# A routed mixture-of-experts stage: x's transposes ahead of the up product, VectorE's order in a step, a smaller block table, and no GpSimd drain at the end

## The reference

```python
x = x + conv_ref(ln_c(x), cfc_w, bn_w, bn_b)       # a gate per image and channel, from mean, max, std and a median
t = to_tokens(x)                                    # 2048 tokens x 512
h = ln_t(t)
logits = h @ router_w.T                             # 8 experts
top_vals, top_idx = top_k(logits, 1)                # one expert for each token
glu = lambda h, wg, wu, wd: silu(h @ wg) * (h @ wu) @ wd
t = t + glu(h, shared_gate.T, shared_up.T, shared_down.T) + sum_e sigmoid(top_vals) * (top_idx == e) * glu(h, w1[e], v1[e], w2[e])
x = from_tokens(t)
```

## Time and profile before

| | us |
|---|---|
| median of three runs | 476.2 |
| span of the profiled execution, first to last instruction | 474.6 |
| TensorE busy | 385.1 |
| VectorE busy | 278.0 |
| ScalarE busy | 160.8 |
| GpSimd busy | 167.9 |

### The profile page before, as it was taken

One profiled execution on the slowest core, in us unless ns is written; L12 is line 12 of the kernel. 1 busy time (PEld: TensorE's weight loads), 2 busy tenths in 40 slices (PEclk: granted clock), 3 DMA queues, 4 the chain that ended last, 5 costly groups with the idle time before them and its releaser, 6 DMA issues.

```text
span 474.6 us, 7391 instructions
## 1 busy us (share of the span) xinstructions
PE 385.1 (81%) x1874; PEld 314.1 (66%) x1875; DVE 278.0 (59%) x499; ACT 160.8 (34%) x262; POOL 167.9 (35%) x203
## 2 busy tenths in 40 slices
PE   2453010389999999999997999999999999999981
PEld 2342010178888888888885778788778788777860
DVE  5985877743645665564679744746447654664330
ACT  4884545221222222232100144515343434343110
POOL 4762911510202022120680658341524152415110
PEclk9655555568999999999999999999999999999997
DMA  8800430110111111111133436974736673633100
GB/s 299 323 1 0 141 124 1 44 46 7 60 44 46 66 44 44 65 46 44 44 113 110 134 120 247 329 247 133 261 107 229 244 265 105 233 151 120 49 24 24
DMA packets 15863, 56.14 MB, mean 118 GB/s; under 512 B 2591, under 2 KB 2591, under 8 KB 12384
## 3 DMA queue, kind: packets, MB, share of 16 engines
q1 hardware_dynamic: 10960, 40.93, 24.0%
q0 software_dynamic: 4880, 14.95, 9.4%
HBM read 43.28 MB, written 13.63 MB: 120 GB/s over the span
## 4 chain that ended last, share of the span: by engine, by line
PE 71%; DVE 13%; issue 5%; ACT 3%; POOL 3%; DVEq 2%; DMA 1%; POOLq 0%
PE GU L1111 41%; PE yb L1111 19%; PE tx L1096 3%; PE th L1103 3%; PE th L1138 3%; DVE tiles L736 2%; DVE search L738 2%; DVEq L247 1%; DVE bn_parts L686 1%; DVE stats L900 1%; DVEq L248 1%; PE yb L1079 1%; PE mb L1089 1%; DVE xT L804 1%; ACT tiles L513 1%
## 5 line engine op out<-in xcount | busy, mean ns | idle before, releaser
L1111 PE MATMUL GU<-w_parts,xT 128*128 (+1 forms) x864 | 220.1, 404 | 4.1 <-issue 2.0
L1111 PEld LDWEIGHTS GU<-w_parts,xT 128*128 128x128 f32 x864 | 160.8, 192 | 41.0 <-issue 9.0
L1111 PE MATMUL yb<-w_parts,hT 128*128 (+1 forms) x432 | 107.3, 397 | 4.9 <-DVE hT L813 4.9
L1111 PEld LDWEIGHTS yb<-w_parts,hT 128*128 128x128 f32 x432 | 79.1, 188 | 22.0 <-issue 6.3
L587 ACT ACTIVATE hT<-th 128x512 fp32r<-128x512 f32 x36 | 21.5, 599 | 171.0 <-PE th L1103 171.0
L448 POOL DMA_INDIRECT out<-x_sb,scatidx x20 | 28.5, 1427 | 104.1 <-DVE x_sb L1010 102.1
L819 DVE TENSOR_TENSOR hidden<-hidden,GU 128x512 f32<-128x512 f32 x36 | 24.8, 688 | 60.5 <-issue 43.6
L577 ACT ACTIVATE xT<-tx 128x512 fp32r<-128x512 f32 x37 | 22.2, 599 | 91.2 <-PE tx L1096 91.2
L501 ACT ACTIVATE w_parts<-w_raw 128x2048 f32 (+1 forms) x27 | 50.7, 1907 | 0.1
L1005 DVE TENSOR_TENSOR w_parts<-w_raw,w_parts 128x2048 f32 x19 | 43.5, 2289 | 6.5 <-ACT w_parts L501 3.0
L404 POOL TENSOR_TENSOR x_rstd<-x_mv,eps 128x1 f32<-128x1 f32 x16 | 3.5, 217 | 117.3 <-DVE x_mv L795 117.3
(11 more groups left out here) (195 smaller groups left out, 386.0 us busy)
## 6 DMA issues: line engine op xcount, KB each, us to landing
w_raw<-weights SPq DMA_DIRECT2D x27, 1024.0 KB, 4.9
x_sb<-x_tok SPq DMA_DIRECT2D x8, 512.0 KB, 7.4
xn_d<-tiles SPq DMA_DIRECT2D x16, 256.0 KB, 2.0
z_d<-x_sb SPq DMA_DIRECT2D x16, 256.0 KB, 2.0
tiles<-xn_d,tokidx POOLq DMA_INDIRECT x21, 4.1
x_sb<-z_d,tokidx POOLq DMA_INDIRECT x20, 5.2
out<-x_sb,scatidx POOLq DMA_INDIRECT x20, 3.8
conv<-conv_par SPq DMA_DIRECT2D x1, 10.0 KB, 9.9
```

What stands on the lines that cost most here:

```text
L1111: last = pe.matmul(dst, left[:, lp, kc, :], wset(q, k, wp, kc), start=(i == 0), stop=(i == 3 * KC - 1))
```

## The change

It does five things.

- `nc.Block(no_gpsimd_drain=True)`.
- TensorE's step: `transpose_x` of block n + 2 moves ahead of the up product of n + 1. The table now gives a set number for this block and the next; slot and counter value are worked out from it in registers (`at % 2`, `at * 3`).
- ScalarE's step: `x_hi` moves ahead of `silu_gate`, and four table entries in place of seven are read behind both. One flag serves GATE and UP.
- VectorE's step: `x_lo` moves ahead of `gated`; three entries in place of seven are read, behind `gated`; the GATE split stands before `add_routed`, the UP split behind it, ahead of DOWN's.
- GpSimd no longer makes the low parts of set 2's gate and up; VectorE makes them between `gated` of block 0 and block 0's step. `block_table` has some instructions fewer.

```diff
-SLOT_COL, READY_COL, SLOT2_COL, READY2_COL = range(4)
-TOTAL_COL = 4
-OTHER_COL, FIRST_COL, LOADED_COL, BEFORE_COL = range(8, 12)
-FLAG_COL, COLS = 12, 16
+SET_COL, SET2_COL, TOTAL_COL = range(3)
+DUE_GU_COL, DUE_DOWN_COL, AT_COL, FIRST_COL, COLS = range(4, 9)
...
-        block = ctx.enter_context(nc.Block())
+        block = ctx.enter_context(nc.Block(no_gpsimd_drain=True))
...
-            return [nc.s_assert_within(v, lowest.get(col, 0), highest.get(col, 1))
-                    for v, col in zip(got, cols)]
+            return [nc.s_assert_within(v, *bounds[col]) if col in bounds else v for v, col in zip(got, cols)]
...
             split_lo(1, DOWN)
-            split_lo(2, GATE)
             pool.wait_ge(z_out, 16 * NT)
             for b in range(RING - 1):
                 gather_z(b)
-            split_lo(2, UP)
             pool.wait_ge(tables, 1)
...
             def step(b, u, j, base):
                 h_hi(b + NT, u % 2)
+                x_hi(b + (NT + 2), u % 2)
                 silu_gate(b + (NT + 1), 1 - u % 2)
-                entries = table_entries(act, b + 1, range(OTHER_COL, FLAG_COL + 3))
-                x_hi(b + (NT + 2), u % 2)
-                next_set(entries)
+                next_set(table_entries(act, b + 1, range(DUE_GU_COL, FIRST_COL + 1)))
...
+            def lo_of(k, at):
+
+                dve.wait_ge(whi, at * 3 + (k + 4))
+                dve.wait_ge(wlo, at * 3 + (k + 3))
+                if isinstance(at, int):
+                    lo, hi = (w_parts[:, (at + 1) % 2, k, part, :, :] for part in (LO, HI))
+                else:
+                    lo, hi = (w_parts[:, ds((at + 1) % 2, 1), k, part, :, :].rearrange("p a k c -> p (a k) c") for part in (LO, HI))
+                dve.tensor_tensor(lo, w_raw[:, k, :, :], hi.bitcast(F32), ALU.subtract).then_inc(wlo, 1)
...
             def step(b, u, j, base):
                 h_lo(b + NT, u % 2)
-                entries = table_entries(dve, b + 1, range(OTHER_COL, FLAG_COL + 3))
+                x_lo(b + (NT + 2), u % 2)
                 gated(b + (NT + 1), 1 - u % 2)
-                x_lo(b + (NT + 2), u % 2)
-                next_set(entries, (GATE, UP))
+                due_gu, due_down, at = table_entries(dve, b + 1, range(DUE_GU_COL, AT_COL + 1))
+                with dve.If(due_gu > 0):
+                    lo_of(GATE, at)
                 add_routed(b + NT, b, u, j * 16 + 16 * (base + 1))
-                next_set(entries, (DOWN,))
+                with dve.If(due_gu > 0):
+                    lo_of(UP, at)
+                with dve.If(due_down > 0):
+                    lo_of(DOWN, at)
...
             dve.wait_ge(tables, 1)
-            next_set(table_entries(dve, 0, range(OTHER_COL, FLAG_COL + 3)), (DOWN,))
+            lo_of(GATE, 1)
+            lo_of(UP, 1)
+            _, due_down, at = table_entries(dve, 0, range(DUE_GU_COL, AT_COL + 1))
+            with dve.If(due_down > 0):
+                lo_of(DOWN, at)
             groups(dve, step, last)
...
-                q, ready, q_after, ready_after = table_entries(pe, b, range(SLOT_COL, READY2_COL + 1))
-                gate_product(n + 1, 1 - u % 2, 1 - u % 2, q_after, ready_after)
+                at, after = table_entries(pe, b, range(SET_COL, SET2_COL + 1))
+                gate_product(n + 1, 1 - u % 2, 1 - u % 2, after % 2, after * 3)
                 transpose_h(n, u % 2)
-                up_product(n + 1, 1 - u % 2, 1 - u % 2, q_after, ready_after)
 
                 pe.wait_ge(xg_in[ahead], j * 16 + 16 * (base + 1 + (u + 2) // RING))
                 transpose_x(n + 2, xg[:, ahead, :])
-                down_product(n, u % 2, q, ready)
+                up_product(n + 1, 1 - u % 2, 1 - u % 2, after % 2, after * 3)
+                down_product(n, u % 2, at % 2, at * 3)
```

More of the change, by code:

```diff
@@ L618, in next_set @@
             def next_set(entries):
[L620 to L626, removed]
+                due_gu, due_down, at, first = entries
+                for ks, due in (((GATE, UP), due_gu), ((DOWN,), due_down)):
+                    with act.If(due > 0):
+                        act.wait_ge(y_done if ks == (DOWN,) else u_done, first + NT)
+                        for k in ks:
+                            act.wait_ge(w_in[k], at * 16 + 32)
+                            split_hi(w_raw[:, k, :, :], w_parts[:, ds((at + 1) % 2, 1), k, HI, :, :].rearrange("p a k c -> p (a k) c"))
             def step(b, u, j, base):
                 h_hi(b + NT, u % 2)
+                x_hi(b + (NT + 2), u % 2)
                 silu_gate(b + (NT + 1), 1 - u % 2)
-                entries = table_entries(act, b + 1, range(OTHER_COL, FLAG_COL + 3))
-                x_hi(b + (NT + 2), u % 2)
-                next_set(entries)
+                next_set(table_entries(act, b + 1, range(DUE_GU_COL, FIRST_COL + 1)))
             def last(b, u, j, base):
@@ L638, in _ @@
             act.wait_ge(tables, 1)
-            next_set(table_entries(act, 0, range(OTHER_COL, FLAG_COL + 3)))
+            next_set(table_entries(act, 0, range(DUE_GU_COL, FIRST_COL + 1)))
             groups(act, step, last)
@@ L977, in block_table @@
                 settle()
-                note(dve.scalar_tensor_tensor(out=ft[:, :, FLAG_COL + GATE], in0=r_b, scalar=0.0, in1=live, op0=ALU.is_equal, op1=ALU.mult))
-                note(dve.scalar_tensor_tensor(out=ft[:, :, FLAG_COL + UP], in0=r_b, scalar=0.0, in1=live, op0=ALU.is_equal, op1=ALU.mult))
+                note(dve.scalar_tensor_tensor(out=ft[:, :, DUE_GU_COL], in0=r_b, scalar=0.0, in1=live, op0=ALU.is_equal, op1=ALU.mult))
                 note(dve.tensor_tensor(fl, fl, r_b, ALU.is_equal))
-                own(dve.tensor_scalar(ei, ei, 1, None, ALU.bitwise_and))
@@ L985, in block_table @@
-                note(dve.memset(ft[:, 0, FLAG_COL:FLAG_COL + 2], 0.0))
-                note(dve.tensor_tensor(ft[:, :, FLAG_COL + DOWN], fl, live, ALU.mult))
-                own(dve.tensor_copy(ft[:, :, OTHER_COL], ei))
-                own(dve.tensor_scalar(ft[:, :, SLOT_COL], ft[:, :, OTHER_COL], -1.0, 1.0, ALU.mult, ALU.add))
-                note(dve.tensor_copy(ft[:, 0:NB - 1, SLOT2_COL:READY2_COL + 1], ft[:, 1:NB, SLOT_COL:READY_COL + 1]))
-                own(dve.tensor_copy(ft[:, NB - 1, SLOT2_COL:READY2_COL + 1], ft[:, NB - 1, SLOT_COL:READY_COL + 1]))
+                note(dve.tensor_copy(ft[:, 0:NB - 1, SET2_COL], ft[:, 1:NB, SET_COL]))
@@ L992, in block_table @@
+                own(dve.tensor_copy(ft[:, NB - 1, SET2_COL:SET2_COL + 1], ft[:, NB - 1, SET_COL:SET_COL + 1]))
+                note(dve.memset(ft[:, 0, DUE_GU_COL:DUE_GU_COL + 1], 0.0))
+                own(dve.tensor_tensor(ft[:, :, DUE_DOWN_COL], fl, live, ALU.mult))
                 note(dve.tensor_copy(tab[0:1, 0:NB, 0:TOTAL_COL + 1], ft[:, :, 0:TOTAL_COL + 1]))
-                own(dve.tensor_copy(tab[0:1, 0:NB, OTHER_COL:FLAG_COL + 3], ft[:, :, OTHER_COL:FLAG_COL + 3]))
+                own(dve.tensor_copy(tab[0:1, 0:NB, DUE_GU_COL:COLS], ft[:, :, DUE_GU_COL:COLS]))
@@ L994, in block_table @@
                 dve.engine_nop().then_inc(tables, 1)
-            def next_set(entries, ks):
-                other, _, _, before, *due = entries
-                for k in ks:
-                    with dve.If(due[k] > 0):
-                        dve.wait_ge(whi, before + (k + 4))
-                        dve.wait_ge(wlo, before + (k + 3))
-                        lo, hi = (w_parts[:, ds(other, 1), k, part, :, :].rearrange("p a k c -> p (a k) c") for part in (LO, HI))
-                        dve.tensor_tensor(lo, w_raw[:, k, :, :], hi.bitcast(F32), ALU.subtract).then_inc(wlo, 1)
+            def lo_of(k, at):
[6 more added lines that the diff above has]
+                dve.tensor_tensor(lo, w_raw[:, k, :, :], hi.bitcast(F32), ALU.subtract).then_inc(wlo, 1)
```

17 lines of the change are left out of this document (6 added, 11 removed).

## The result

The changed kernel takes 463.44 us (median of four runs, 461.75 to 466.02) against 476.04 of the kernel before: ratio 0.9756, interval 0.9721 to 0.9792. The profiled execution has a span of 464.3 us and a time of 466.02, so 1.7 us lie between; the forecast had counted 1.6. The forecast was 466.5 (464.2 to 471.8).

A forecast was written before the change was run, and what follows sets the result against it. TensorE's work was taken as the bound. From 474.6 us: minus 5.06 drain, 6.27 stalls and 0.34 start, plus 1.15 and 0.8 new stalls, gives 464.9; with 1.6 between span and time 466.5, range 464.2 to 471.8.

The forecast's parts named there:

- The drain: At the block's end: leaving out GpSimd's DRAIN takes 5.06 us off the path; bounds nothing to 5.06.
- The stalls of the steps: Routed stage, 19 steps in 179.74 us against 173.47 at the quiet 9.13: 6.27 us of stalls counted as removed.
- The stall at block 0: Set 2's splits on VectorE ahead of block 0's h_lo delay its down product: 1.15 us added, bounds 0.1 to 3.4.
- an entry costs 0.28 us: VectorE's table read: each entry priced at 0.28 us, so four fewer save 1.1 us per step.
- The 0.8 us at the changes under conditions: Last two of six steps before a new expert: gates 0.2 and 0.5 late, 0.8 us added, bounds 0 to 1.7.
- The eight transposes in a row: TensorE's step, x transposes right behind h's: no change that could be priced, plus and minus 0.4 us over 19.
- The start: First step, where TensorE idles 0.34 us at 279.00: fewer table entries and operations gain 0.34 us.
- The signs: Trace signs: no GpSimd drain row, no x_lo waits, h_lo wait about 1 us, last h transposes about 454.4.
- Rival 1: Block's end: the drain's time comes back, span shrinks but measured time doesn't; 471.6 us, chance 0.15.
- Rival 2: Steps: the stalls move, for example to h_lo behind both splits, and the 6.27 us stay; 472.8 us, chance 0.08.
- Rival 3: TensorE's queue: remainder worked out again at each of 464 weight addresses, so slower; 523 us, chance 0.03.
- GpSimd's gathers: Gathers of z beside set 2's splits: nothing added; by the skill's lockout rule about 1 us longer.

The follow-up runs named there:

- the two runs: Kernel before without the GpSimd drain: 468.64 us against 473.87, ratio 0.9893. Changed kernel with the drain put back: 467.36 us, 4.9 above the changed kernel.
- the old order: Changed kernel with up product again ahead of the x transposes (TensorE) and silu ahead of x's high part (ScalarE): 472.31 us, ratio 0.9963.
- the second: Changed kernel measured again with no edit, against the kernel before: 462.42 us against 473.87, ratio 0.9762.
- The order alone: Kernel before with only TensorE's x transposes ahead of up and ScalarE's x high part ahead of silu: 473.14 us against 474.43, ratio 0.9979.
- bare flags alone: Kernel before with no bounds assertion on the table's three flags, all else unaltered: 472.28 us against 474.43, ratio 0.9955.

## Why the prediction was right, and where its steps were not

**The drain** was sized right: 5.06 forecast, 5.08 in the traces (10.57 to 5.49 us behind the last matmul), 5.2 and 4.9 in the times. Its own row gave the size. That the time doesn't come back elsewhere took the two runs.

**The stalls of the steps.** 6.27 us were forecast to go and 1.95 to come. In the profiled executions the steps lost 6.78 us net, block 0's early start apart. Three terms were off, and their errors lie on one side:
- The stall at block 0 was put at 1.15 us and measured 0.31 (a distance of 0.54 between starts where 0.23 is usual; the whole step is 0.46 longer than a quiet one). The failing figure was "an entry costs 0.28 us". That is the price of an entry's bounds assertion, not of the entry. The two bare flags come free, which is 0.56 us, and the first of the two table reads took 1.00 us for 1.30. So h_lo ran at 285.00 right behind the splits in place of 285.6.
- The 0.8 us at the changes under conditions didn't come. Splits started 5.6 to 6.0 us after the h transposes in place of 6.2, which fits the same misjudged price, and no issue gap is left.
- The eight transposes in a row were put at nothing, with 0.4 us either way, and brought 1.1: a quiet step is 9.07 for 9.13, confirmed by the old order's 9.13. Why they are cheaper was not tried.

**The start** of 0.34: block 0's h transposes come 11.49 us after the gate product of the block's own (270.56 to 282.05), 12.08 before, so 0.59. The 0.47 that this execution was late ahead of that is not shown to be the change's.

With these the sum is 5.08 + 6.78 + 0.59 - 0.27 (last block) = 12.18 us, where 6.78 is the net of the three terms above and the stalls that went. The times have 12.6 in the first comparison and 11.45 in the second. In the profiled execution 0.47 us were lost ahead of block 0 and 1.44 at the last down product by the clock, which leaves 10.27, as the spans have it (474.57 and 464.30). That its time of 466.02 stands by the forecast of 466.5 is luck. The median lies below the stated range, at 463.44, because three terms were too dear. (The forecast's own upper end adds up to 469.7 and not 469.5; nothing hangs on it.)

**The signs.** The drain's row is gone and the time stayed 1.7 over the span, as said. No gate product waits for x_lo. The last h transposes came at 452.17, not about 454.4. The wait near 285.4 is there at a third of its size, and the issue gaps near 405 and 425 are not.

**The reason for the stalls was named in part.** The forecast laid the gain on VectorE's order ("more matters the order: h_lo, x_lo, gated product, then the read"). The runs show it makes no difference in the changed kernel (170.07 and 170.09), and alone costs 11 us or more. What carries the steps is TensorE's place for the x transposes together with the shorter read. The order alone gives 1.3 us, bare flags alone 2.15 us, the rest without the order is 1.6 to 2.9 us worse in the stretch than the kernel before, and all together 5.5 to 6.8 us better. That the shorter read is the second half follows by elimination: VectorE's order, the split order and set 2's place were each undone in the changed kernel and moved the stretch by 0.6 us at most. No run had the order and the short read without the rest, and TensorE's and ScalarE's orders moved together in every run, so what each of these two gives isn't shown. The forecast looked at x's low part as the only customer of the early transposes. The second customer is ScalarE's high parts of the next set, which wait in line behind x's high part and the read. It passed over them: of ScalarE it says only that silu moves behind x_hi "and nothing wants it before 3.9". They start 4.3 us after the h transposes in the kernel before and 2.4 in the changed one.

**Rivals.** Rival 1 falls (two runs). Rival 2 was the true danger: "h_lo, now behind both splits at each change of expert" is just what happens when TensorE's and ScalarE's order is undone, and there it costs 8.4 us in the stretch. Rival 3 falls: the address operations keep 464 instances and 0.046 us.

**GpSimd's gathers.** The forecast added nothing for them. One of them first in line might have pushed the gate split back; it came 0.28 us behind the split, and it was the gathers that were held, harmlessly. Order of time in the changed kernel:

```profile
280.20 4.68 DVE L989 TENSOR_TENSOR w_parts<-w_raw,w_parts 128x2048 fp32r<-128x2048 f32 x2
280.48 2.85 POOL L438 DMA_INDIRECT x_sb<-z_d,tokidx  x1 [6.04 <-DMA z_d<-x_sb]
...
283.63 2.07 POOL L438 DMA_INDIRECT x_sb<-z_d,tokidx  x1 [0.30 <-issue]
...
286.01 0.95 POOL L438 DMA_INDIRECT x_sb<-z_d,tokidx  x1 [0.30 <-issue]
```

Two gathers that begin while a split runs take 2.85 and 2.07 us, the one after them 0.95. It is so for all 15 indirect transfers of this trace that begin while a split runs: they end 0.8 to 0.9 us after it. In the earlier trace rows the gather had begun ahead of the split. By the Trainium skill's "SBUF — State Buffer", section on the two sides, the later of the two waits: these rows agree, for the gather as for the scatter. The other half of it, that a GpSimd operation in progress holds the split, no row here shows for a gather: the split of the earlier trace rows ran its usual 2.29 us though it began behind one.

## What to carry to other kernels

When a step has one transposition or copy that feeds a chain on another engine, ask for everything that stands in line behind that chain's first operation, not only for its own reader: here weight splits for the next expert sat behind it. Parts of a hand-written schedule can be worth little or be harmful alone and pay together, so price them as a set, and by a stretch of the trace that the clock doesn't touch. Here a bounds assertion on a register cost queue time as an operation does (0.28 us on VectorE), and a GpSimd drain behind transfers already waited for cost 5 us that came back nowhere else when it was left out.

## What the runs showed of the hardware that was not expected

- Eight transposes in a row cost TensorE 0.06 us less per step than two groups of four with a product between.
- GpSimd's DRAIN took 5.06 us with its last scatter's completion already awaited, in the kernel before and in the changed one with the drain, where GpSimd made two splits fewer.
- Executions of one kernel differ by 3 us with the granted clock outside the steps; the last down product alone takes 3.02 us at 1.00 or 4.48 where the clock fell to 0.50 in its course, behind the same wait of TensorE of about 2 us.
- A table read by VectorE's queue took 0.33 us with the engine idle (282.66 in the kernel before) and 1.04 in the median beside its own engine's work. One read of 0.33 stands beside a running split (284.16 in the changed kernel), so work under way isn't the whole cause, and why it reaches 1.93 was not tried.
